# Two graph layers and two expert layers on one core: the graph layer's end goes tile by tile, residual sums move into waits, the last extra expert is tested first, and one chunk of the second recurrent expert goes ahead of a turn

## What is computed

```python
x = x + L0_gnn(layernorm(x), edges, ...)        # 3 diffusion steps over a 256 x 256 adjacency
x = x + L0_ffn(layernorm(x), ...)               # 8 experts, top 2, gelu, 512 -> 1024 -> 512
x = x + L1_gnn(layernorm(x), edges, edge_attr, ...)
x = x + L1_ffn(layernorm(x), ...)               # 8 recurrent experts, top 2, 512 -> 3*512 -> 512

# L1_gnn, with h the normalised tokens and 4352 edges (34 tiles of 128)
m = relu(concat(h[src], edge_attr) @ W1.T + b1) @ W2.T + b2
agg = segment_sum(m, dst)
i_r, i_z, i_n = split(agg @ W_ih.T + b_ih)
h_r, h_z, h_n = split(h @ W_hh.T + b_hh)
r, z = sigmoid(i_r + h_r), sigmoid(i_z + h_z)
n = tanh(i_n + r * h_n)
h_new = (1 - z) * n + z * h
out = h + gamma * (h_new - run_mean) * rsqrt(run_var + eps) + beta
```

## Time and profile before

| what | value |
|---|---|
| time, median of 3 runs | 480.96 us (480.10 to 481.13) |
| the profiled execution's own time | 481.92 us |
| its span | 480.10 us |
| PE busy, mean granted clock | 443.1 us (92%), 0.955 |
| DVE, ACT, POOL busy | 397.9 us (83%), 281.6 us (59%), 104.4 us (22%) |
| moved | 115.67 MB, mean 241 GB/s |

### The profile page before, as it was taken

How to read it: one execution, slowest core, us unless ns; L and a number is a source line. 1 busy time by engine, 2 the same in 40 slices (tenths; PEclk the granted TensorE clock), 3 DMA queues, 4 the chain that set the end, 5 groups by cost and what they waited for, 6 DMA issues and landing times.

```text
span 480.1 us, 6137 instructions
## 1 busy us (share of the span) xinstructions
PE 443.1 (92%) x2208; PEld 354.5 (74%) x2208; DVE 397.9 (83%) x645; ACT 281.6 (59%) x306; POOL 104.4 (22%) x128
## 2 busy tenths in 40 slices
PE   3989899999999988899999998988999999999795
PEld 2655578888887868587899987656788888887674
DVE  8989768988989774777999888887798998979754
ACT  3245348787777753533444346345887888849541
POOL 5641000110010031157876200020001111000300
PEclk9999789999999997899999999979899999999797
DMA  7931545999998836788777244134789999967701
GB/s 251 305 130 44 186 173 211 348 335 360 358 367 311 339 148 253 286 303 296 203 201 248 72 156 155 41 137 175 284 297 348 342 404 363 364 226 289 281 2 45
DMA packets 25780, 115.67 MB, mean 241 GB/s; under 512 B 7036, under 2 KB 7708, under 8 KB 14864
## 3 DMA queue, kind: packets, MB, share of 16 engines
q1 hardware_dynamic: 18400, 93.90, 53.1%
q0 software_dynamic: 7056, 21.26, 13.4%
q10 hardware_dynamic: 288, 0.03, 0.1%
HBM read 108.63 MB, written 6.55 MB: 240 GB/s over the span
## 4 chain that ended last, share of the span: by engine, by line
PE 70%; DVE 14%; DMA 7%; ACT 4%; issue 3%; POOL 1%; DVEq 0%; ACTq 0%; SPq 0%; POOLq 0%
PE bank L1507 14%; PE bank L1508 14%; PE bank L1512 14%; PE bank L1883 3%; PE bank L1885 3%; PE bank L1500 3%; PE bank L1501 2%; PE bank L1502 2%; PE bank L1521 2%; PE bank L1772 2%; PE bank L1710 2%; DVE wlo L930 2%; DMA gath<-node_rows,src_i 2%; DMA raw<-in_weights_dram 2%; DMA y_tok<-y_rows,row_i 1%
## 5 line engine op out<-in xcount | busy, mean ns | idle before, releaser
L930 DVE TENSOR_TENSOR wlo<-raw,whi 128x2048 fp32r<-128x2048 f32 x73 | 165.3, 2287 | 19.5 <-ACT whi L675 18.7
L675 ACT ACTIVATE whi<-raw 128x2048 fp32r<-128x2048 f32 x73 | 137.6, 1914 | 11.0 <-PE bank L1852 6.4
L1507 PE MATMUL bank<-whi,xe_hi 128*128 128x512 f32 x192 | 79.1, 412 | 1.9 <-ACT xe_hi L704 1.4
L1508 PE MATMUL bank<-wlo,xe_hi 128*128 128x512 f32 x192 | 77.7, 405 | 0.0
L1512 PE MATMUL bank<-whi,xe_lo 128*128 128x512 f32 x192 | 52.6, 395 | 0.0
L1507 PE MATMUL bank<-whi,hT_hi 128*128 128x512 f32 (+1 forms) x124 | 50.2, 408 | 2.1 <-ACT hT_hi L732 2.1
L1508 PE MATMUL bank<-wlo,hT_hi 128*128 128x512 f32 (+1 forms) x124 | 48.4, 394 | 0.0
L617 POOL DMA_INDIRECT xg<-node_rows,idx x12 | 11.8, 985 | 160.8 <-DVE idx L1193 160.8
L650 POOL DMA_INDIRECT gath<-node_rows,src_i x34 | 42.0, 1234 | 14.9 <-DVE mp L1424 9.5
L1507 PEld LDWEIGHTS bank<-whi,xe_hi 128*128 128x128 f32 x192 | 37.1, 193 | 10.9 <-ACT xe_hi L704 1.9
L1508 PEld LDWEIGHTS bank<-wlo,xe_hi 128*128 128x128 f32 x192 | 37.2, 194 | 8.1
(11 more groups left out here) (307 smaller groups left out, 858.2 us busy)
## 6 DMA issues: line engine op xcount, KB each, us to landing
raw<-in_weights_dram SPq DMA_DIRECT2D x85, 1024.0 KB, 6.5
y_rows<-y_sb POOLq DMA_DIRECT2D x16, 256.0 KB, 6.0
ea<-in_ea_dram SPq DMA_DIRECT2D x8, 256.0 KB
node_rows<-xn POOLq DMA_DIRECT2D x4, 256.0 KB, 2.6
gath<-node_rows,src_i POOLq DMA_INDIRECT x34
x<-in_x_dram SPq DMA_DIRECT2D x1, 512.0 KB, 4.0
gw<-in_L_ffn_gw_dram SPq DMA_DIRECT2D x1, 512.0 KB, 10.6
node_rows<-A_sb POOLq DMA_DIRECT2D x2, 256.0 KB, 4.7
```

Source lines behind the costliest of these rows:

```text
L675: act.activation(whi[n % SPL][:, :, :], raw[n % RAW][:, :, :], ACT.Copy).then_inc(hi_cut, 1)
L930: dve.tensor_tensor(wlo[n % SPL][:, :, :], raw[n % RAW][:, :, :], whi[n % SPL][:, :, :].bitcast(f32), ALU.subtract).then_inc(lo_cut, 1)
L1507: pe.matmul(ps, xh[:, blocks + k, :], whi[w % SPL][:, k, cs], start=first and k == 0, stop=False)
L1508: pe.matmul(ps, xh[:, blocks + k, :], wlo[w % SPL][:, k, cs], start=False, stop=False)
```

## The change

- FFN gating: `low_tokens` goes from behind the ranking to between two weight cuts. Fill: 2 matmuls more ahead of the wait for the hidden layer, 7 instead of 5 ahead of the mask, 4 instead of 2 ahead of the gather.
- FFN end: SP may load W1 of the graph layer once the first extra chunk was cut (before, all four). ACT and DVE cut W1 (`next_layer`) ahead of the turned activations of the last job, and no longer between the two halves of its output. On PE each further job's "last" form is tested first, with the "followed" form behind it. The matmuls that add output biases go behind the first extra product where a further job exists. Fill ahead of the next layer: 8 instead of 14.
- Graph layer: Whh of the candidate is multiplied ahead of the edges and that of the update gate late, into the bank in which Wih of the update gate is added; two ACT copies and two DVE additions go. `base(0)` goes into the wait for the first gathered edge rows, `base(1)` to just behind the last message cut. Wih is multiplied tile by tile: three gates of tile 0, then three gates of tile 1; the DVE and ACT chains follow per tile. The first LSTM chunk is cut by DVE in two halves between them. Tile 0 is normalised and transposed during the end of tile 1; the fill of 24 matmuls becomes 5, the transposes of tile 0, and 14.
- LSTM: the first in-chunk of the second expert goes ahead of the transpose of the first expert's h.

```diff
-GNN_ORDER = [("gnn", "W1")] + [("gnn", "Whh", g) for g in range(3)] + [("gnn", "W2")] \
+GNN_ORDER = [("gnn", "W1")] + [("gnn", "Whh", g) for g in (0, 2, 1)] + [("gnn", "W2")] \
...
+                if last_first:
+                    with eng.If(number < e + 2 - E):
+                        job(e, False)
+                    with eng.If(number > e + 1 - E):
+                        job(e, True)
+                        run_from(e + 1)
                     return
...
+            def jobs_cut(run, number, chunks):
+
                 for job in range(MORE):
                     with sp.If(number > job):
-                        sp.wait_ge(run.more_lo, EC * (job + 1))
+                        sp.wait_ge(run.more_lo, EC * job + chunks)
...
-            more(ffn)
+            number = more(ffn)
+            jobs_cut(ffn, number, 1)
             main(GNN_ORDER[0:1])
             sp.wait_ge(y_in, 16 * 2 * NT)
+            jobs_cut(ffn, number, EC)
...
+                xT_copy(2 * nth - 1, xnT, None if nth == 1 else first + 2 * SPL + 3)
+                cut_to(SPL if nth == 1 else CHUNK[LSTM_ORDER[0]] + SPL)
...
+                both_tiles(act, n, g1["gi_ps"], 2, CHUNK[("gnn", "Wih", 1)])
+                act.activation(rz[:, n, 1, :], B[4 + n][:, :], ACT.Sigmoid, scale=-1.0).then_inc(g1["u"], 1)
+                if n == 0:
+                    cut_to(first + 2 * SPL + 1)
...
+            def cut_half(n, half):
+                if half == 0:
+                    dve.wait_ge(hi_cut, n + 1)
+                ks = slice(half * KB // 2, (half + 1) * KB // 2)
+                ins = dve.tensor_tensor(wlo[n % SPL][:, ks, :], raw[n % RAW][:, ks, :],
+                                        whi[n % SPL][:, ks, :].bitcast(f32), ALU.subtract)
+                if half == 1:
+                    ins.then_inc(lo_cut, 1)
+                    done[0] += 1
...
+                if nth == 1:
+                    cut_to(SPL - 2)
+                    low_tokens()
+                cut_to(SPL - 1 if nth == 1 else CHUNK[LSTM_ORDER[0]] + 2)
...
-                        if h == 1:
-                            next_layer()
...
+                    else:
+                        next_layer()
...
+                if t == 0:
+                    dve.wait_ge(g1["a_out"], 16 * NT)
+                    base(0)
...
+            base(1)
             dve.wait_ge(g1["sum_ps"], ET)
...
+            for n in range(NT):
+                reset(n)
+                if n == 1:
+                    cut_half(first + 2 * SPL, 1)
+                update(n)
+                candidate(n)
+                if n == 0:
+                    cut_half(first + 2 * SPL, 0)
+                else:
+                    normalise(3, (0,))
+                tokens(n)
+                moments(n)
...
+                turn_x(2 * nth - 1, range(NT) if nth == 1 else (1,))
...
+                    keep_busy(B[0], 2)
...
-                keep_busy(B[0], 5)
+                keep_busy(B[0], 7 if nth == 1 else 5)
...
+                            pe.wait_ge(run.h_ok, 1 if e == 1 and run.layer else 2 * e)
...
+                        if e == 1 and c == 0 and run.layer:
+                            turn_h(0, 3)
...
-                keep_busy(B[0], 2)
+                keep_busy(B[0], 2 if run.layer else 4)
...
-                    biases(run.layer + 1, not followed)
+                    if not followed:
+                        biases(run.layer + 1, True)
                     second_product(E - 1)
                     if followed:
                         first_product(E)
+                        biases(run.layer + 1, False)
...
-            keep_busy(B[2], 14)
+            keep_busy(B[2], 8)
...
-                ps = B[(6, 2, 4)[g] + n]
-                if g == 1:
+                ps = B[(6, 4, 2)[g] + n]
+                if g == 2:
...
-            for g in range(3):
-                q = CHUNK[("gnn", "Wih", g)]
-                has_chunk(q)
-                for n in range(NT):
-                    ps = B[(6, 2, 4)[g] + n]
+            for n in range(NT):
+                for g in range(3):
+                    q = CHUNK[("gnn", "Wih", g)]
+                    if n == 0:
...
-            keep_busy(B[0], 24)
+            keep_busy(B[0], 5)
+            pe.wait_ge(g1["u"], NT)
+            turn_x(3, (0,))
+            keep_busy(B[0], 14)
```

More of the change, by code:

```diff
@@ L319, in __call__, with further_jobs @@
                 self.eng.wait_ge(self.s, self.n)
-        def further_jobs(eng, number, before, job):
+        def further_jobs(eng, number, before, job, last_first=False):
             def run_from(e):
@@ L689, in cut_to, with xT_copy @@
                     done[0] += 1
-            def xT_copy(layer, dst):
+            def xT_copy(layer, dst, cut):
                 for n in range(NT):
+                    if n and cut:
+                        cut_to(cut)
                     act.wait_ge(xt_ps, NT * layer + n + 1)
@@ L881, in gh_copy @@
             def gh_copy(g, n):
-                both_tiles(act, n, g1["gh_ps"], g + 1, CHUNK[("gnn", "Whh", g)])
-                act.activation(gh[:, n, g, :], B[(6, 2, 4)[g] + n][:, :], ACT.Copy).then_inc(g1["gh_sb"], 1)
+                both_tiles(act, n, g1["gh_ps"], 2, CHUNK[("gnn", "Whh", g)])
+                act.activation(gh[:, n, g, :], B[2 + n][:, :], ACT.Copy).then_inc(g1["gh_sb"], 1)
             both_tiles(act, 1, None, 0, CHUNK[("gnn", "Whh", 0)])
@@ L904, in _ @@
                                ACT.Copy).then_inc(g1["ag_hi"], 1)
-            gh_copy(2, 1)
             cut_to(first + 2 * SPL)
-            cut_to(first + 2 * SPL + 1)
             for n in range(NT):
@@ L948, in moments, with normalise @@
                 dve.tensor_scalar(var_eps[:, n:n + 1], mv[:, n, 1:2], EPS, None, ALU.add).then_inc(var_ok, 1)
-            def normalise(layer):
-                for n in range(NT):
+            def normalise(layer, tiles=range(NT)):
+                for n in tiles:
                     dve.wait_ge(rstd_ok, NT * layer + n + 1)
@@ L1065, in gating @@
             def gating(nth):
-                normalise(2 * nth - 1)
+                normalise(2 * nth - 1, range(NT) if nth == 1 else (1,))
                 if nth == 1:
@@ L1457, in _, with reset, update @@
                                   ag_hi[:, 2 * b:2 * b + 2, :].bitcast(f32), ALU.subtract).then_inc(g1["ag_lo"], 1)
-            base(1)
             cut_to(first + 2 * SPL)
-            cut_to(first + 2 * SPL + 1)
-            for n in range(NT):
+            dve.wait_ge(g1["gh_sb"], NT)
+            def reset(n):
                 dve.wait_ge(g1["r"], n + 1)
-                dve.wait_ge(g1["gh_sb"], NT + n + 1)
-                ins = dve.tensor_tensor(rz[:, n, 0, :], rz[:, n, 0, :], gh[:, n, 2, :], ALU.mult)
-            link(ins)
-            for n in range(NT):
-                both_tiles(dve, n, g1["gi_ps"], 2, CHUNK[("gnn", "Wih", 1)])
-                dve.tensor_tensor(rz[:, n, 1, :], B[2 + n][:, :], gh[:, n, 1, :], ALU.add)\
-                   .then_inc(g1["z_in"], 1)
-            for n in range(NT):
+                link(dve.tensor_tensor(rz[:, n, 0, :], rz[:, n, 0, :], gh[:, n, 2, :], ALU.mult))
+            def update(n):
                 dve.wait_ge(g1["u"], n + 1)
@@ L1522, in keep_busy, with turn_x @@
                               iota_b[:, :].unsqueeze(1).to_broadcast([P, 2, T]), start=True, stop=True)
-            def turn_x(layer):
-                for n in range(NT):
+            def turn_x(layer, tiles=range(NT)):
+                for n in tiles:
                     pe.wait_ge(xn_ok, NT * layer + n + 1)
@@ L1820, in job @@
                         last_sum(e)
-                further_jobs(pe, number, before, job)
+                further_jobs(pe, number, before, job, True)
             keep_busy(B[0], 24)
@@ L1856, in whh @@
                 else:
-                    ins.then_inc(chunk_used, 2 if g == 2 else 1)
-            for g in range(2):
+                    ins.then_inc(chunk_used, 2 if g == 1 else 1)
+            for g in (0, 2):
                 for n in range(NT):
@@ L1894, in _ @@
             pe.wait_ge(g1["mp"], ET)
-            whh(2, 0)
+            whh(1, 0)
             pe.wait_ge(g1["s1_hi"], 2)
```

61 lines of the change are left out of this document (25 added, 36 removed).

## The result

After the change the median is 479.8 us (20 runs, 475.11 to 486.54) against 481.59 for the kernel before beside it (20 runs, 478.82 to 484.57). The ratio is 0.9939, 95% interval [0.9915, 0.9964]: 2.9 us faster, between 1.7 and 4.1. The medians here are over all runs (they lie 1.8 us apart), while the ratios leave out as slow every run that is over 1.5% above the fastest of its kernel, 5 of the 20 here and 6 of the 12 of e8. I had forecast 469.8 and a range from 466.5 to 475.9, so the prediction was wrong: right in sign, nearly four times too large, and outside its range.

The account below looks back on a forecast made before the run. PE, busy 92% of the span, was taken as the bound. Gains A 4.4, B 2.0, C 3.8 and D 1.0 sum to 11.2 us: 470.7 from the profiled 481.92, or 469.8 on the median's basis; range 466.5 to 475.9.

Parts of the forecast that it names:

- B: End of the FFN: W1 cut and skipped block leave the critical places; gain 2.0 us, bounds 0.5 and 3.3.
- rival 3: FFN end: W1 lands 3 us late and ACT stalls PE; B is 0.1, time 471.7 us; chance 0.05.
- The skipped block is now behind the last sums, where the fill starts up to 1.85 us late: Step of B, FFN end: 8 fill matmuls start up to 1.85 us late, ending about when tokens are normalised.
- A: FFN gating: 0.55 us from the earlier gather plus 3.85 from the clock staying up; gain 4.4 us.
- Behind it the first transposes wait for ACT, which waits for PE, so they move along: Step of A, behind the FFN gating: first transposes move along with the gain; DVE's cuts are ready before PE asks.
- Rival 1: FFN gating: the clock falls as before; A is 0.3, time 473.9 us; chance 0.20.
- C: End of the second graph layer: 1.6 us from earlier Wih plus 2.2 from a shorter tail; gain 3.8 us.
- rival 2: Graph layer's end: DVE becomes the bound; C keeps only 1.6, time 472.0 us; chance 0.08.
- D: LSTM: 13 matmuls of the next chunk fill PE's idle; 1.7 us, or 0.3 if the clock falls; 1.0 taken.
- PE has then waited 2.0 us: Step of D, LSTM: PE waits 2.0 us and its transpose moves from 351.70 to 350.0 us.
- Rival 4: Slower: with less fill PE enters W1's and Whh products at 1.2 GHz and stays; over 482 us; chance 0.02.
- Rival 5: Experts wait for weights and swallow the early gains; A and D vanish, time 475.2 us; chance 0.05.

Follow-up runs that it names:

- e8: The changed kernel with the four `base(0)` operations ahead of the aggregates again, as before the change: 481.86 us, ratio to before 0.9946.
- e1: The changed kernel with the old order of tests on PE (followed form first): 476.94 us, ratio to before 0.9889.
- e9: The changed kernel with three edits joined (old test order, later read of the number, nine fill matmuls in the LSTM's pause): 469.21 us, ratio to before 0.9743.
- e3: The kernel before with only the new test order (last form first), its 14 fills kept: 488.27 us, ratio to before 1.0143.
- e4: The changed kernel with the LSTM's chunk of the second expert behind the first turn again: 479.13 us, ratio to before 0.9960.
- e5: The changed kernel with VectorE's read of the number of extra jobs two steps later in the FFN: 475.7 us, ratio to before 0.9856.
- e6: The changed kernel with nine fill matmuls in the LSTM's new pause: 477.32 us, ratio to before 0.9928.
- e11: The changed kernel with the eight fills at the FFN's end put ahead of the jump over the skipped block: 480.8 us, ratio to before 1.0013.
- e12: e9 with the fill matmuls of the two gatings as before the change, six fewer: 471.16 us, ratio to before 0.9837.
- e2: The changed kernel without the 8 fill matmuls behind the FFN's last sums: 477.46 us, ratio to before 0.9941.

## Why the prediction was wrong

**B is where it failed most: 4.1 us.** Up to the x addition the steps hold in kind. PE's wait at the skipped block went, and the last job's transposes came 2.0 us earlier against T2 (forecast 1.8). But the order of the tests isn't what gave this: e1, with the old order, has them 1.6 earlier. ACT cut W1 at 176.93 and stalled nobody (rival 3 falls). The row gathers did not get faster: DVE's sums start at 186.14, 104.7 behind T2 (104.8 before), so the W1 cut's 2.2 was all that there was to gain. The x addition came 1.66 sooner, not 2.2 to 3.0, since PE ran its last sums at half clock; in e1 and e9, at the full clock, it is 2.55 to 2.57. The step that failed is "The skipped block is now behind the last sums, where the fill starts up to 1.85 us late". I had taken the stall's price from the part of it that showed in the earlier trace rows, where it ran beside a wait for ACT. Behind the last sums nothing hides it: 4.76 in after, 4.74 in e3, 5.33 to 5.78 in e4, e5, e6 and e8. And it isn't one price that moves with the skipped code: what counts is when the load of instructions starts against the wait that could cover it. I also had the fill end "at about the time the tokens are normalised" at either clock; it started 1.45 behind them. The Trainium skill, Runtime: NRT & Kernel Launch, section Instruction fetch mechanics, names a taken branch to a page that isn't held as a stall, and says that going on to the next block in straight code is mostly hidden. The traces agree that PE waits for a fetch: a piece of 16 KB on an instruction queue lies in each of these stalls, with PE going on 2.81 to 2.84 us behind its start in seven kernels. On straight code this case is less kind than the page: the 3.07 us in e11 have such a piece in them too (from 199.11), in code without a branch. The 2.98 that comes and goes between e9 and e12 shows that the load's place hangs on how many instructions lie ahead; by what rule isn't shown.

**A: 3.0 us, and again a wait, not the clock.** The clock stayed up from 54 to 64, here and in all twelve kernels with the low part moved, and the gather came at 55.51 (55.55 forecast). The step that failed is "Behind it the first transposes wait for ACT, which waits for PE, so they move along". They wait for `slot_read` too, and VectorE reaches the slot numbers only behind the chain of the extra experts and its read of a register, 1.30 us with nothing busy. Before, PE at half rate came later than that. e5 takes the read away from the path and A is 4.19. In six of the seven kernels like after the third expert's rows then come late as well, which can cost more: T2 is 83.65 in e8, later than before. Rival 1 falls as it was put, since the clock fell only behind the new wait. The rule of the Trainium skill named under A, strictly taken, had the gating itself fall; neither after nor e12 shows that.

**C was right:** 3.44 of 3.8. The first Wih product moved 1.7 (1.6 forecast), the tail 1.7 (2.2). DVE's slack ahead of tile 1's candidate was 0.44, 0.35 forecast, so it never bound, and rival 2 falls.

**D: the step "PE has then waited 2.0 us" missed the same wait.** The pause moved from the first turning to the second and became 2.92, because DVE writes `idx` at 348.53, behind two cuts, two activations' products and a low part. PE was ahead in work and not in time. With the clock up this is worth 0.6, with a fall behind it it costs 1.0. The fall came in three of six traces that have this unfilled pause (after, e1, e8; not e2, e5, e11); what decides it isn't shown.

**The rest.** "The other edits come to 0" holds as far as the stages show. Rival 4 came at a small size: low stretches arose behind the FFN's end. Rival 5 is refuted: PE never waited long for weights. That e9 lands near my 469.8 doesn't bear the forecast out: 5.2 of its 12.5 us against before lie in the last stage, where no term was, 1.9 of B's gain are lost again in the edge stage (in waits of 1.50 for DVE's `ea_lo` and 1.00 with no open wait), and it takes three edits that I hadn't foreseen as needed.

## What to carry to other kernels

A stall that shows in a trace may be only what other waits didn't cover: before moving it, ask what it costs with no cover, and what stands behind it. When PE stands still with no open wait, look in the DMA view for a piece on an instruction queue. When a wait is shortened, list every semaphore that the next instruction waits for, with the time each is ready at; the one that isn't last today is the next bound. With a clock that falls behind pauses, compare stages with equal clock (the one from the last edge sum to the logits repeated to 0.01 us in eleven kernels) and judge the whole by medians over many runs.

## What the runs showed of the hardware

The same program spreads, in part by how much of it runs at half clock: the 20 runs of after go from spans of 473.3 and 473.9 at mean clocks of 0.972 and 0.979 to 484.7 at 0.953. A low stretch that an edit removes often comes back at another seam: after lost 10.2 us at 54 and gained 10.5 at 189.5, and e1 lost these and had 13.5 instead of 6.7 at the second gating. TensorE stood still for 3.07 us in the middle of eight like transposes, 2 us after the last thing that they wait for was there, with a piece of 16 KB on an instruction queue from 199.11. Behind a skipped block of code, where nothing else held it, PE went on 2.81 to 2.84 us behind the start of such a piece. And a read of one number into a VectorE register cost 1.30 us of that engine's time, 0.79 of it seen in its sequencer.
